# A pre-norm attention and mixture-of-experts layer: three output products taken in 32 bits, and the second norm of batch 0 turned by TensorE

## The chip, the cores and the metric

One Trainium2 chip; the kernel runs on one core of it. The metric is device time in microseconds (us) for one execution, the median of three runs.

## The reference

One transformer layer over `x` of 8 batches x 256 tokens x 256 features. Linear attention first, then a mixture of experts, each behind a layer norm:

```python
n = layernorm(x)
q, k, v = n @ Wq.T + bq, n @ Wk.T + bk, n @ Wv.T + bv
phi_q, phi_k = elu(q) + 1, elu(k) + 1
context = phi_q * cumsum(phi_k * v, axis=tokens) * 0.25
x = x + context @ Wo.T + bo
h = layernorm(x)
top2, idx = top_k(h @ router_w, 2);  scores = softmax(top2)
routed = sum over the two experts e of score * (silu(h @ w1g[e]) * (h @ w1u[e])) @ w2[e]
shared = silu(h @ w_gate) * (h @ w_up) @ w_down
out = x + routed + shared
```

There are 8 experts with an inner width of 512; the shared expert has 1024. All inputs and outputs are float32.

## The kernel before, in words

Every engine runs a list of steps in an order written out by hand; steps wait for each other on counting semaphores. A batch (index `i`, 0 to 7) is two tiles of 128 tokens. For each batch the steps are: first norm (`stats1`, `norm1`, `normed1`), turning the normed rows so that features lie on partitions, `project` (keys, values, queries), `exps` on ScalarE, `keys`, `sums` (the running sum), `queries` and `context` on VectorE, the output product `attend_out` on TensorE, `residual` on VectorE, second norm (`stats2`, `moments2`, GpSimd's `pow2`, VectorE's four small steps `newton2`, ScalarE's `normed2`), the turning of its result, `route` (router product), `gate_up` and `down` (the shared expert), `logits`, `ranks`, `slots`. `to_rows` scatters each token's row to a table in HBM. From about 195 us on the 36 expert blocks are worked through in one loop.

Products are made of float16 halves: each operand `a` is `a_h + a_l`, and a product is `a_h*w_h + a_h*w_l + a_l*w_h`. An output product of one batch, `attend_out(i)`, is therefore 12 matmuls of 256 columns, and its operand `cx` (the context, float32, stored in place over `rq`) must first be split: ScalarE writes `cx_h` (`context_hi`), VectorE subtracts and writes `cx_l` (`context_lo`). The attention weights lie in `wa_h` and `wa_l`, multiplied by `WS` = 64; their float32 original stays in `stage_att`.

The output bias `bo` is added to `xs` (the residual rows) by an accumulating DMA that GpSimd issues, `add_bo(i)`, for each batch ahead of `residual(i)`, which waits for it on `xbo0` or `xbo1`.

Turning: for batches 0 to 2 the first norm's rows are turned by TensorE (`turn_first`, then `turned_hi` on ScalarE and `turned_lo` on VectorE). All others, and the second norm of every batch, go as float16 halves (`row_hi2`, `row_lo`) through a DMA transpose that SP issues (`turn2`).

The head of the order, up to the first `route`, on TensorE is: `project(0)`, `project(1)`, 16 matmuls of ones that nobody reads (`warm(16)`), `attend_out(0)`, `turn_first(2)`, `project(2)`, `warm(10)`, `attend_out(1)` with a `warm(10)` inside, `warm(22)`, `route(0)`, `gate_up(0, 0)`. SP's queue holds `turn2(0)` ahead of the loads of the first three expert parts.

Of the kernel before, what the change touches and what calls it, by code (L numbers as in the profile page):

```python
# [26 lines left out]
P = 128  # L27
# [5 lines left out]
def layer_kernel(nc, x, w_att, w_bias, w_bo, w_shared, w_expert, out):  # L33
# [33 lines left out]
    with ExitStack() as ctx:  # L67
# [23 lines left out]
        def router_w(w):  # L91
# [15 lines left out]
        row_f = sb("row_f", [P, 1])  # L107
        spare = sb("spare", [P, 1])

# [103 lines left out]
        lent_down = lent[:, 2 * W1:2 * EW].rearrange("p (c s n) -> p c s n", s=2, n=D)  # L213
        ya = [xs[:, n, :] for n in range(NY)]

        names = """x0_in x1_in x2_in x_in att_k_in att_k_hi att_k_lo att_v_in att_v_hi att_v_lo att_in bias_in bo_in up_in gate_in down_in
            ex_in0 ex_in1 ex_in2 att_hi att_lo sh_hi sh_lo ex_hi ex_lo
            const_pool const_dve bias_done out_saved
            first0 first1 ln1_step pln ln2_step mv1_done ve1 ve2 pln2 float_done pow1 pow2 norm1_done norm2_done xn1 xn2 xbo0 xbo1
            t1 h1_done l1_done xT1_in h2_done l2_done xT2_in  # L220
# [47 lines left out]

        ON_DVE = 4


# [62 lines left out]
        def _(sp):  # L334
# [45 lines left out]

            turn2(0)
            for p in range(3):
# [75 lines left out]
        def _(pool):  # L458
# [182 lines left out]
            pool.wait_ge(S["bo_in"], 16)  # L641
            add_bo(0)
            add_bo(1)
# [139 lines left out]
        def _(pe):  # L783
# [47 lines left out]
            def attend_out(i):  # L831


                pe.wait_ge(S["cxh_done"], i + 1)
                if i >= 1:
                    pe.wait_ge(S["x1_done"], i)
                wh, wl = att_w(wa_h, 3), att_w(wa_l, 3)
                for s, (a, w) in enumerate(((cx_h, wh), (cx_h, wl), (cx_l, wh))):
                    if s == 2:
                        if i == 1:  # L840
                            warm(10)
                        pe.wait_ge(S["cxl_done"], i + 1)
                    for t in range(TB):
                        for k in range(KC):
                            ins = pe.matmul(bT[:, t * D:(t + 1) * D], a[:, k, t * P:(t + 1) * P], w[:, k, :],  # L845
                                            start=s + t + k == 0, stop=s == 2 and k == KC - 1, skip_group_check=True)
                ins.then_inc(S["wo_ps"], 1)

            def route(i):

                pe.wait_ge(S["xT2_in"], 16 * TB * (i + 1))
# [111 lines left out]
            warm(10)  # L963
# [13 lines left out]
            project(3, "k")  # L977
            attend_out(2)
            project(3, "qv")
# [149 lines left out]
        def _(act):  # L1129
            def exps(i, which="kq"):  # L1130

                for name, ready, e, r, m, ed, rd, used in (("k", "k_ps", ek, rk, 1, "ek_done", "rk_done", "kvs_done"),
                                                           ("q", "q_ps", eq, rq, 0, "eq_done", "rq_done", "cxl_done")):
                    if name not in which:
                        continue
                    src = projected(i, name)
                    act.wait_ge(S[ready], i + 1)
                    if i >= 1:
                        act.wait_ge(S[used], i)
                    for c in range(KC):  # L1140
                        act.activation(e[:, c, :], src[:, c * L:(c + 1) * L], ACT.Exp, bias=bias[:, m, c:c + 1],
                                       scale=1.0 / WS).then_inc(S[ed], 1)
                    for c in range(KC):
                        act.activation(r[:, c, :], src[:, c * L:(c + 1) * L], ACT.Identity, bias=bias1[:, m, c:c + 1],
                                       scale=1.0 / WS).then_inc(S[rd], 1)

            def load_exp():
                act.activation(spare[:], bias[:, 0, 0:1], ACT.Exp)

            def load_silu():  # L1150
                act.activation(spare[:], bias[:, 0, 0:1], ACT.Silu)

            def context_hi(i):
                act.wait_ge(S["cx_done"], i + 1)
                if i >= 1:
                    act.wait_ge(S["wo_ps"], i)
                act.activation(cx_h[:], cx, ACT.Copy).then_inc(S["cxh_done"], 1)
# [18 lines left out]
            def turned_hi(i):  # L1176

                act.wait_ge(S["t1"], i + 1)
                if i == 2:
                    act.wait_ge(S["q_ps"], 1)  # L1180
                act.activation(turned1(i)[:, 0:KC, :].rearrange("p k l -> p (k l)"), turn_bank(i)[:], ACT.Copy
                               ).then_inc(S["h1_done"], 1)

            def normed2(i):

                act.wait_ge(S["norm2_done"], 2 * (i + 1))
                if i >= 1:
                    act.wait_ge(S["l2_done"], i)
# [6 lines left out]
            def row_hi2(i):  # L1195
                act.wait_ge(S["xn2"], TB * (i + 1))
                if i >= 2:
                    act.wait_ge(*saved_before(i))
                    act.wait_ge(S["xT2_in"], 16 * TB * (i - 1))
                act.activation(rows2[i % 2][:, :, 0:D], xn[1][:], ACT.Copy).then_inc(S["h2_done"], 1)  # L1200
# [82 lines left out]
            load_exp()  # L1283
            context_hi(2)
            act_hi(0, 3)
# [134 lines left out]
        def _(dve):  # L1420
# [76 lines left out]
            def keys(i):  # L1497

                dve.wait_ge(S["ek_done"], KC * (i + 1))
                dve.wait_ge(S["rk_done"], KC * (i + 1))  # L1500
                dve.scalar_tensor_tensor(out=phik, in0=ek, scalar=1.0, in1=rk, op0=ALU.min, op1=ALU.max
                                         ).then_inc(S["phik_done"], 1)
                dve.wait_ge(S["phik_done"], i + 1)
                dve.wait_ge(S["v_ps"], i + 1)
# [25 lines left out]
            def context_lo(i):  # L1530
                dve.wait_ge(S["cxh_done"], i + 1)
                dve.tensor_tensor(cx_l[:], cx, cx_h[:], ALU.subtract).then_inc(S["cxl_done"], 1)

            def residual(i):

                dve.wait_ge(S["wo_ps"], i + 1)
                dve.wait_ge(S[f"xbo{i % 2}"], 16 * (i // 2 + 1))
                dve.scalar_tensor_tensor(out=xs_of(i), in0=bT[:].rearrange("p (t d) -> p t d", t=TB), scalar=1.0 / (WS * CS),
                                         in1=xs_of(i), op0=ALU.mult, op1=ALU.add).then_inc(S["x1_done"], 1)
# [88 lines left out]
            def turned_lo(i):  # L1628
                dve.wait_ge(S["h1_done"], i + 1)
                dve.tensor_tensor(turned1(i)[:, KC:2 * KC, :].rearrange("p k l -> p (k l)"), turn_bank(i)[:],  # L1630
                                  turned1(i)[:, 0:KC, :].rearrange("p k l -> p (k l)"), ALU.subtract).then_inc(S["l1_done"], 1)

            turned_lo(0)
            att_lo(slice(KC * D, 2 * KC * D), "att_v_hi", "att_v_lo")
# [58 lines left out]
            logits(1, 0)  # L1693
            context_lo(2)
            logits(1, 1)
# [263 lines left out]
```

## Time and profile before

| what | value |
|---|---|
| time, median of 3 runs (lowest to highest) | 355.33 us (355.15 to 355.61) |
| the profiled execution's own time | 356.11 us |
| its span, first to last instruction | 354.1 us |
| mean granted TensorE clock over the span | 0.996 |
| busy: TensorE / VectorE / ScalarE / GpSimd | 340.8 / 236.5 / 215.1 / 195.2 us |

Busy is the time an engine had an instruction in work; idle time of an engine counts only where another one waits for it. The span leaves out some 2.0 us of the profiled execution that lie around the first and last instruction.

### The profile page before, as it was taken

What the parts mean: (1) busy time and instruction counts of PE and PEld (TensorE: products, weight loads), DVE (VectorE), ACT (ScalarE), POOL (GpSimd) and SP (SyncE); (2) the same over time, 40 slices, a digit from 0 to 9 for tenths busy, and PEclk for the clock granted to TensorE, in tenths of its full rate; (3) what the DMA queues carried; (4) which work ended last, traced back from release to release, by engine and by line L of the source; (5) the groups of instructions that cost most, each with busy time, mean ns of one, the idle gap of its engine ahead of it and who ended that gap; (6) DMA issues with size and microseconds to landing.
All of it is one profiled execution on the core that took longest, in us unless ns stands there. A gap on an engine that the chain in (4) does not pass through costs nothing.

```text
span 354.1 us, 9236 instructions
## 1 busy us (share of the span) xinstructions
PE 340.8 (96%) x2971; PEld 257.5 (73%) x2971; DVE 236.5 (67%) x587; ACT 215.1 (61%) x391; POOL 195.2 (55%) x282
## 2 busy tenths in 40 slices
PE   7988989999999999999999999999999999999993
PEld 7877868888888898898988465656655556666662
DVE  4978998899989888887788554454544543334441
ACT  3669858787897977856536354454545544554551
POOL 4768986767785848356056444343443535443335
PEclk9999999999999999999999999999999999999998
DMA  7985342456774755725785346866496775765650
GB/s 197 381 213 103 137 108 45 132 144 209 128 228 105 140 185 136 197 92 152 234 266 134 91 76 98 105 86 92 68 114 94 89 113 80 104 106 90 94 71 8
DMA packets 77468, 46.43 MB, mean 131 GB/s; under 512 B 61040, under 2 KB 72560, under 8 KB 77040
## 3 DMA queue, kind: packets, MB, share of 16 engines
q1 hardware_dynamic: 63088, 35.08, 40.5%
q0 software_dynamic: 9664, 10.71, 19.0%
q10 hardware_dynamic: 4672, 0.07, 0.9%
q8 instruction: 26, 0.43, 0.5%
q14 instruction: 18, 0.15, 0.2%
HBM read 19.09 MB, written 12.97 MB: 91 GB/s over the span
## 4 chain that ended last, share of the span: by engine, by line
PE 73%; DVE 10%; DMA 6%; issue 4%; ACT 3%; POOL 1%; SPq 1%; POOLq 0%; DVEq 0%; ACTq 0%
PE bU L1065 13%; PE bG L1065 13%; PE bD L942 8%; PE bQ L1090 6%; PE bV L1090 6%; PE bG L238 6%; PE bU L238 6%; DMA xs<-bo 3%; PE bK L238 3%; PE bV L238 3%; PE bK L1045 2%; DMA bo<-in_w_bo 2%; DVE ab L1547 2%; PE bT L942 2%; PE bT L845 2%
## 5 line engine op out<-in xcount | busy, mean ns | idle before, releaser
L1547 DVE SCALAR_TENSOR_TENSOR ab<-bU,sg 128x512 f32<-128x512 f32 x64 | 44.1, 690 | 66.2 <-PE bU L1065 47.2
L773 POOL DMA_INDIRECT out_y<-xs,dst_row x32 | 49.6, 1551 | 60.1 <-DVE dst_row L1880 26.4
L1207 ACT ACTIVATE sg<-bG 128x512 f32<-128x512 f32 x64 | 37.9, 593 | 44.0 <-PE bG L1065 27.0
L1065 PE MATMUL bG<-we,work 128*128 (+1 forms) x216 | 52.6, 380 | 0.0
L1065 PE MATMUL bU<-we,work 128*128 (+1 forms) x216 | 52.6, 379 | 0.0
L571 POOL DMA_INDIRECT x_rows<-rows,slot_u x32 | 40.7, 1273 | 18.2 <-issue 10.7
L1374 ACT ACTIVATE ws_h<-ab 128x512 f16<-128x512 f32 x36 | 22.7, 629 | 41.6 <-DVE ab L1547 41.6
L1865 DVE TENSOR_TENSOR ws_h<-ab,ws_h 128x512 f16<-128x512 f32 x36 | 24.9, 692 | 20.8 <-ACT ws_h L1374 20.2
L1214 ACT ACTIVATE ah<-ab 128x512 f16<-128x512 f32 x32 | 20.1, 629 | 25.4 <-DVE ab L1547 21.3
L1065 PEld LDWEIGHTS bG<-we,work 128*128 128x128 f16 (+1 forms) x216 | 20.7, 99 | 19.3 <-issue 1.6
L1065 PEld LDWEIGHTS bU<-we,work 128*128 128x128 f16 (+1 forms) x216 | 19.9, 99 | 17.3
L1090 PE MATMUL bQ<-wd,ws_l 128*128 (+1 forms) x216 | 26.8, 273 | 0.1
L1090 PE MATMUL bV<-wd,ws_l 128*128 (+1 forms) x216 | 26.8, 273 | 0.0
L1090 PEld LDWEIGHTS bQ<-wd,ws_l 128*128 128x128 f16 (+1 forms) x216 | 21.0, 99 | 7.0 <-issue 1.9
L1090 PEld LDWEIGHTS bV<-wd,ws_l 128*128 128x128 f16 (+1 forms) x216 | 21.1, 99 | 6.7 <-issue 1.7
L768 POOL DMA_INDIRECT out_y<-xs,half_dst x8 | 12.3, 1543 | 23.9 <-issue 13.1
L238 PE MATMUL bG<-xT,ws_h 128*128 128x256 f16 x144 | 24.5, 273 | 0.0
L238 PE MATMUL bU<-xT,ws_h 128*128 128x256 f16 x144 | 24.5, 273 | 0.0
L1552 DVE TENSOR_TENSOR al<-ab,ah 128x512 f16<-128x512 f32 x32 | 21.7, 679 | 1.9 <-ACT ah L1214 1.8
L1381 ACT ACTIVATE ws_l<-bK 128x512 f16<-128x512 f32 x36 | 21.3, 592 | 0.6 <-PE bK L1045 0.6
L1603 DVE SCALAR_TENSOR_TENSOR we<-stage,we 128x1024 f16<-128x1024 f32 x16 | 19.5, 1219 | 0.8 <-ACT we L1234 0.8
L1045 PEld LDWEIGHTS bK<-ident,ws_h 128*128 128x128 f16 x144 | 10.6, 98 | 9.9 <-issue 1.6
(327 smaller groups left out, 822.4 us busy)
## 6 DMA issues: line engine op xcount, KB each, us to landing
stage<-in_w_expert SPq DMA_DIRECT2D x24, 512.0 KB
we<-in_w_shared SPq DMA_DIRECT2D x3, 1024.0 KB, 12.6
xs<-bo POOLq DMA_DIRECT2D x8, 256.0 KB, 4.3
out_y<-xs SPq DMA_DIRECT2D x8, 256.0 KB
xs<-in_x SPq DMA_DIRECT2D x1, 1280.0 KB, 19.4
x_rows<-we SPq DMA_DIRECT2D x9, 134.0 KB
xs<-in_x SPq DMA_DIRECT2D x3, 256.0 KB, 4.1
work<-x_rows SPq DMA_TRANSPOSE x40
```

The source lines that it names most:

```text
L238: ins = pe.matmul(dst, a(c), b(c), start=s == 0 and c == 0, stop=s == 2 and c == n - 1)
L571: pool.indirect_dma_start(xrows, bass.IndirectOffsetOnAxis(ap=slot_u[q][:, k, t:t + 1], axis=0), rows2[q][:, t, :].bitcast(U16), None).the ...
L773: pool.indirect_dma_start(out_rows, bass.IndirectOffsetOnAxis(ap=dst_row[:, b:b + 1], axis=0), ya[b % NY], None, bounds_check=NT * P - 1, ...
L942: ins = pe.matmul(dst[:, t * D:(t + 1) * D], a[:, at:at + P], w[:, 2 * f + c, :], start=f + s + t + c == 0, stop=f == NP - 1 and s == 2 an ...
L1065: ins = pe.matmul(dst[t * n:(t + 1) * n, :], x2[:, hi * KC + k, t * n:(t + 1) * n], w[t][lo][:, k, half, :], start=s == 0 and k == 0, stop ...
L1090: ins = pe.matmul(dst[t * m:(t + 1) * m, :], a[:, c, t * m:(t + 1) * m], w[t][:, c, lo, :], start=s == 0 and c == 0, stop=s == 2 and c == ...
L1207: act.activation(sg[q][:], src[:], ACT.Silu, scale=1.0 / WS).then_inc(S["sg_done"], 1)
L1374: act.activation(ar_h[n], ab[b % 2][:], ACT.Copy).then_inc(S["ah_done"], 1)
L1381: act.activation(aT_h[n].rearrange("p c l -> p (c l)"), bK[:], ACT.Copy).then_inc(S["ath_done"], 1)
L1547: dve.scalar_tensor_tensor(out=ab[q][:], in0=src[:], scalar=1.0 / WS, in1=sg[q][:], op0=ALU.mult, op1=ALU.mult).then_inc(S["a_done"], 1)
L1552: dve.tensor_tensor(al[f][:], ab[f % 2][:], ah[f][:], ALU.subtract).then_inc(S["al_done"], 1)
L1865: dve.tensor_tensor(ar_l[n], ab[b % 2][:], ar_h[n], ALU.subtract).then_inc(S["al_done"], 1)
```

## The change

The output products of batches 0, 1 and 2 are made from the unsplit float32 `cx` and the float32 weights in `stage_att`: 4 matmuls instead of 12 (`attend_whole`). Their `context_hi` and `context_lo` go. Batch 0's bias is laid into the same accumulator by two matmuls of one row (`add_bo_first`), in place of its accumulating DMA. Batch 0's second norm is turned by TensorE (`turn_second`), ScalarE (`turned2_hi`) and VectorE (`turned2_lo`) instead of the DMA transposes; its float16 rows are still written for `to_rows`. The order of the head follows on every engine. `WHOLE` is 3.

```diff
@@ SP's queue
-            turn2(0)
             for p in range(3):
                 load_part(p)
             turn2(1)
@@ GpSimd
             pow1(0)
+            pool.memset(cs_row, CS).then_inc(S["cs_row"], 1)
...
-            add_bo(0)
             add_bo(1)
             norm1(2)
@@ TensorE, new functions
+            def add_bo_first():
+                pe.wait_ge(S["bo_in"], 16)
+                pe.wait_ge(S["cs_row"], 1)
+                pe.wait_ge(S["l1_done"], 2)
+                for t in range(TB):
+                    pe.matmul(bT[:, t * D:(t + 1) * D], cs_row, bo[0:1, :], start=t == 0, stop=False, skip_group_check=True)
+
+            def attend_whole(i):
+                pe.wait_ge(S["att_in"], 16)
+                pe.wait_ge(S["cx_done"], i + 1)
+                if i >= 1:
+                    pe.wait_ge(S["x1_done"], i)
+                w = att_w(stage_att, 3)
+                for t in range(TB):
+                    for k in range(KC):
+                        ins = pe.matmul(bT[:, t * D:(t + 1) * D], cx[:, k, t * P:(t + 1) * P], w[:, k, :],
+                                        start=i >= 1 and t + k == 0, stop=k == KC - 1, skip_group_check=True)
+                ins.then_inc(S["wo_ps"], 1)
+
+            def turn_second():
+                pe.wait_ge(S["xn2"], TB)
+                pe.wait_ge(S["rq_done"], KC * 2)
+                for t in range(TB):
+                    for k in range(KC):
+                        ins = pe.transpose(bD[:, k * L + t * P:k * L + (t + 1) * P], xn[1][:, t, k * P:(k + 1) * P], ident[:])
+                ins.then_inc(S["t2"], 1)
@@ TensorE, order
             project(1)
-            warm(16)
-            attend_out(0)
+            add_bo_first()
+            warm(4)
+            attend_whole(0)
             turn_first(2)
             warm(8, bQ)
-            project(2)
-            warm(10)
-            attend_out(1)
-            warm(22)
+            project(2, "kv")
+            turn_second()
+            project(2, "q")
+            attend_whole(1)
             route(0)
             pe.wait_ge(S["const_pool"], 6)
             gate_up(0, 0)
+            warm(24, bD)
             gate_up(0, 1)
...
             project(3, "k")
-            attend_out(2)
+            attend_whole(2)
             project(3, "qv")
@@ ScalarE, exps: a later batch's queries wait for the product that reads cx
-                    if i >= 1:
+                    if i >= 1 and name == "k":
                         act.wait_ge(S[used], i)
+                    elif 1 <= i <= WHOLE:
+                        act.wait_ge(S["wo_ps"], i)
+                    elif i > WHOLE:
+                        act.wait_ge(S[used], i - WHOLE)
@@ ScalarE, order
             exps(1, "k")
-            context_hi(0)
             normed1(2)
             turned_hi(2)
-            exps(1, "q")
             act.wait_ge(S["up_in"], 16)
             shared_hi(1, 0)
+            exps(1, "q")
             normed2(0)
             row_hi2(0)
-            context_hi(1)
+            turned2_hi()
             act.wait_ge(S["down_in"], 16)
             shared_hi(2, 0)
             exps(2, "k")
-            shared_hi(0, 1)
             exps(2, "q")
             silu(0, 0)
-            shared_hi(1, 1)
+            shared_hi(0, 1)
             act_hi(0, 0)
             silu(1, 1)
+            shared_hi(1, 1)
             normed2(1)
...
-            context_hi(2)
@@ VectorE, order (keys is cut into mapped_keys and key_values)
             context(0)
-            context_lo(0)
-            keys(1)
+            shared_lo(0, 0)
+            mapped_keys(1)
             residual(0)
             stats2(0)
             moments2(0)
+            key_values(1)
             turned_lo(2)
-            sums(1)
             for k in range(4):
                 newton2(0, k)
+            sums(1)
             queries(1)
             context(1)
+            turned2_lo()
+            shared_lo(1, 0)
             row_lo(1, 0)
-            shared_lo(0, 0)
-            context_lo(1)
-            shared_lo(1, 0)
             dve.wait_ge(S["x_in"], 16)
...
             logits(0, 2)
+            shared_lo(2, 0)
             swiglu(0, 0)
-            shared_lo(2, 0)
...
-            context_lo(2)
```

## Rows read from the trace of the kernel before

**Rows 1.** Stretch, busy us of PE, PEld, DVE, ACT, POOL, granted clock, DMA share, GB/s.

```profile
20.00:30.00 10.00, 7.81 (x84) 6.76 (x82) 7.97 (x19) 6.29 (x13) 6.67 (x17) 1.00 0.64 156
...
54.00:64.00 10.00, 10.00 (x98) 8.64 (x97) 9.33 (x25) 8.38 (x18) 6.37 (x15) 1.00 0.30 52
...
195.00:345.00 150.00, 149.59 (x1087) 90.36 (x1086) 70.08 (x206) 74.07 (x141) 63.40 (x57) 1.00 0.65 92
345.00:355.00 10.00, 3.40 (x31) 2.38 (x28) 1.38 (x2) 1.90 (x4) 4.62 (x3) 0.82 0.10 11
```

**Rows 2.** TensorE's waits from 54 us on: total us, times, longest.

```profile
PE bK L1045 <- ACT ws_h L1374: 0.4, 2, 0.2
```

**Rows 3.** The chain that ended last, to 60 us: start, us, what.

```profile
12.11 10.21 DMA xs<-bo
...
24.80 1.75 POOL y L511
...
31.23 2.51 DMA xT<-rows
```

**Rows 4.** Timeline of TensorE: start, length, line, tiles, count, idle before.

```profile
18.33 1.06 PE L786 MATMUL bR<-ones 128*128 128x128 f16 x16
...
20.94 0.60 PE L795 MATMUL bR<-ident,xn 128*128 128x128 f32 x4
...
34.10 1.03 PE L909 MATMUL bG<-xT,ws_h 128*128 128x256 f16 x8
...
50.85 0.39 PE L238 MATMUL bK<-xT,wa_h 128*128 128x256 f16 x2 [0.83 <-DMA xT<-rows]
...
52.52 0.61 PE L845 MATMUL bT<-wa_h,cx_h 128*128 128x256 f16 x4 [0.18 <-ACT cx_h L1157]
...
53.84 0.38 PE L238 MATMUL bQ<-xT,wa_h 128*128 128x256 f16 x2
```

**Rows 5.** Groups by shape: count, busy us, mean ns of one, idle before.

```profile
L795 PEld LDWEIGHTS bT<-ident,xn 128*128 128x128 f32 x8 | 0.8, 141 | 0.6 <-DVE xn L1456 0.6
```

**Rows 6.** Timeline of VectorE.

```profile
18.05 0.69 DVE L1527 SCALAR_TENSOR_TENSOR work<-work 128x512 f32<-128x512 f32 x1
...
22.42 0.69 DVE L1538 SCALAR_TENSOR_TENSOR xs<-bT,xs 128x512 f32<-128x512 f32 x1 [0.62 <-DMA xs<-bo]
...
24.81 1.22 DVE L1512 TENSOR_TENSOR_SCAN work<-keep,work 128x512 f32<-128x512 f16 x1
26.57 0.16 DVE L1472 SCALAR_TENSOR_TENSOR nt<-y 128x2 f32<-128x2 f32 x1 [0.55 <-POOL y L511]
...
29.14 0.69 DVE L1495 TENSOR_TENSOR rows<-xn,rows 128x512 f16<-128x512 f32 x1 [0.48 <-ACT rows L1200]
29.75 1.22 DVE L1609 SCALAR_TENSOR_TENSOR ws_l<-we,ws_h 128x1024 f16<-128x1024 f32 x1
30.89 0.68 DVE L1532 TENSOR_TENSOR cx_l<-work,cx_h 128x512 f16<-128x512 f32 x1
...
36.99 0.69 DVE L1547 SCALAR_TENSOR_TENSOR ab<-bU,sg 128x512 f32<-128x512 f32 x1 [0.64 <-PE bU L909]
...
45.38 0.73 DVE L1492 TENSOR_TENSOR rows<-xn,rows 128x512 f16<-128x512 f32 x1 [0.28 <-ACT rows L1174]
...
51.11 0.69 DVE L1527 SCALAR_TENSOR_TENSOR work<-work 128x512 f32<-128x512 f32 x1
```

**Rows 7.** Timeline of ScalarE.

```profile
36.24 1.05 ACT L1238 ACTIVATE ws_h<-we 128x1024 f16<-128x1024 f32 x1
37.71 0.63 ACT L1214 ACTIVATE ah<-ab 128x512 f16<-128x512 f32 x1 [0.42 <-DVE ab L1547]
...
39.54 1.09 ACT L1192 ACTIVATE xn<-xs,shift,rstd 128x256 f32<-128x256 f32 x2 [0.71 <-DVE shift L1486]
```

**Rows 8.** Timeline of GpSimd.

```profile
36.89 0.71 POOL L511 TENSOR_TENSOR y<-ve,minus_half 128x2 f32<-128x2 f32 x1
```

More of the change, by code:

```diff
@@ L107, in layer_kernel @@
         row_f = sb("row_f", [P, 1])
-        spare = sb("spare", [P, 1])
+        spare = sb("spare", [P, 2])
         xs = sb("xs", [P, NT, D])
@@ L214, in layer_kernel @@
         ya = [xs[:, n, :] for n in range(NY)]
+        cs_row = sg[1][0:1, 0:P]
         names = """x0_in x1_in x2_in x_in att_k_in att_k_hi att_k_lo att_v_in att_v_hi att_v_lo att_in bias_in bo_in up_in gate_in down_in
@@ L218, in layer_kernel @@
             const_pool const_dve bias_done out_saved
-            first0 first1 ln1_step pln ln2_step mv1_done ve1 ve2 pln2 float_done pow1 pow2 norm1_done norm2_done xn1 xn2 xbo0 xbo1
+            first0 first1 ln1_step pln ln2_step mv1_done ve1 ve2 pln2 float_done pow1 pow2 norm1_done norm2_done xn1 xn2 xbo0 xbo1 cs_row t2 h2_turned l2_turned
             t1 h1_done l1_done xT1_in h2_done l2_done xT2_in
@@ L269, in layer_kernel @@
         ON_DVE = 4
+        WHOLE = 3
         def ln2_at(i):
@@ L847, in attend_out @@
                 ins.then_inc(S["wo_ps"], 1)
-            def route(i):
-                pe.wait_ge(S["xT2_in"], 16 * TB * (i + 1))
+            def add_bo_first():
[8 more added lines that the diff above has]
+                if i >= 1:
+                    pe.wait_ge(S["x1_done"], i)
+                w = att_w(stage_att, 3)
[11 more added lines that the diff above has]
+                ins.then_inc(S["t2"], 1)
+            def route(i):
+                if i == 0:
+                    pe.wait_ge(S["h2_turned"], 1)
+                    pe.wait_ge(S["l2_turned"], 1)
+                else:
+                    pe.wait_ge(S["xT2_in"], 16 * TB * i)
                 if i >= 1:
@@ L1147, in load_exp @@
             def load_exp():
-                act.activation(spare[:], bias[:, 0, 0:1], ACT.Exp)
+                act.activation(spare[:, 0:1], bias[:, 0, 0:1], ACT.Exp)
             def load_silu():
-                act.activation(spare[:], bias[:, 0, 0:1], ACT.Silu)
+                act.activation(spare[:, 1:2], bias[:, 0, 0:1], ACT.Silu)
             def context_hi(i):
                 act.wait_ge(S["cx_done"], i + 1)
-                if i >= 1:
+                if i > WHOLE:
                     act.wait_ge(S["wo_ps"], i)
@@ L1182, in turned_hi, with turned2_hi @@
                                ).then_inc(S["h1_done"], 1)
+            def turned2_hi():
+                act.wait_ge(S["t2"], 1)
+                act.activation(xT2[0][:, 0:KC, :].rearrange("p k l -> p (k l)"), bD[:], ACT.Copy).then_inc(S["h2_turned"], 1)
             def normed2(i):
                 act.wait_ge(S["norm2_done"], 2 * (i + 1))
+                if i == 1:
+                    act.wait_ge(S["t2"], 1)
                 if i >= 1:
@@ L1198, in row_hi2 @@
                     act.wait_ge(*saved_before(i))
-                    act.wait_ge(S["xT2_in"], 16 * TB * (i - 1))
+                if i >= 3:
+                    act.wait_ge(S["xT2_in"], 16 * TB * (i - 2))
                 act.activation(rows2[i % 2][:, :, 0:D], xn[1][:], ACT.Copy).then_inc(S["h2_done"], 1)
@@ L1497, in keys, with mapped_keys @@
             def keys(i):
+                mapped_keys(i)
+                key_values(i)
+            def mapped_keys(i):
                 dve.wait_ge(S["ek_done"], KC * (i + 1))
@@ L1502, in keys, with key_values @@
                                          ).then_inc(S["phik_done"], 1)
+            def key_values(i):
                 dve.wait_ge(S["phik_done"], i + 1)
@@ L1530, in context_lo @@
             def context_lo(i):
-                dve.wait_ge(S["cxh_done"], i + 1)
+                dve.wait_ge(S["cxh_done"], i - WHOLE + 1)
                 dve.tensor_tensor(cx_l[:], cx, cx_h[:], ALU.subtract).then_inc(S["cxl_done"], 1)
@@ L1536, in residual @@
                 dve.wait_ge(S["wo_ps"], i + 1)
-                dve.wait_ge(S[f"xbo{i % 2}"], 16 * (i // 2 + 1))
-                dve.scalar_tensor_tensor(out=xs_of(i), in0=bT[:].rearrange("p (t d) -> p t d", t=TB), scalar=1.0 / (WS * CS),
+                if i >= 1:
+                    dve.wait_ge(S[f"xbo{i % 2}"], 16 * ((i + 1) // 2))
+                dve.scalar_tensor_tensor(out=xs_of(i), in0=bT[:].rearrange("p (t d) -> p t d", t=TB),
+                                         scalar=1.0 / (CS if i < WHOLE else WS * CS),
                                          in1=xs_of(i), op0=ALU.mult, op1=ALU.add).then_inc(S["x1_done"], 1)
@@ L1631, in turned_lo, with turned2_lo @@
                                   turned1(i)[:, 0:KC, :].rearrange("p k l -> p (k l)"), ALU.subtract).then_inc(S["l1_done"], 1)
+            def turned2_lo():
+                dve.wait_ge(S["h2_turned"], 1)
+                dve.tensor_tensor(xT2[0][:, KC:2 * KC, :].rearrange("p k l -> p (k l)"), bD[:],
+                                  xT2[0][:, 0:KC, :].rearrange("p k l -> p (k l)"), ALU.subtract).then_inc(S["l2_turned"], 1)
             turned_lo(0)
```

8 lines of the change are left out of this document (2 added, 6 removed).

## The prediction

> **What bounds the kernel now.** Read the busy time by stretch first. From 54 to 64 us TensorE is busy 10.00 of 10 us, in the expert loop 149.59 of 150 [rows 1], and its waits from 54 us on come to one entry of 0.4 us [rows 2]. From there the time is TensorE's work, so a change ahead of 54 us is worth what it shifts the moment at which this dense stream begins, plus what it takes out of the stream. From 20 to 30 us TensorE is busy 7.81 of 10, part of it with products of ones: the head is bound by a chain of small steps.
>
> The chain of waits shows it [rows 3]: batch 0's bias DMA takes 10.21 us from 12.11 and ends after the product it is added to; GpSimd's power takes 1.75; the DMA transpose 2.51. VectorE's row at 22.42 says the same: 0.62 idle, ended by that DMA [rows 6]. The dense part starts with `gate_up(0, 0)` at 34.10, but one last time TensorE waits on others: 0.83 for a transpose at 50.85 and 0.18 for ScalarE's `cx_h` at 52.52 [rows 4]. The end of `attend_out(2)`, 53.84, is therefore my yardstick.
>
> **The price of a 32-bit product.** No row has one. `attend_out(2)` runs 12 float16 matmuls of 256 columns from 52.52 to 53.84 [rows 4]: 0.11 us each, 1.32 in all. Lower bound: four 32-bit transposes of 128 columns took 0.60 us, what four float16 matmuls of 256 take (0.61, both with the tail of the last) [rows 4], so two passes over the columns, 0.22 for 256 columns, 0.88 for a product of four. Upper bound while passes alone count: a full product of two operands of two halves has four partial products where the split form has three, 1.32 x 4 / 3 = 1.76. Beyond that, weight loads: a 32-bit one took 141 ns [rows 5]; one for each of 16 passes, overlapped, makes 2.26, and not overlapped 16 x (0.11 + 0.141) = 4.0. I take 1.76: this is a true product, not a copy, and the row nearest to it is the split product. The bias's two matmuls are half of that, 0.88 (0.44 to 2.0). The Trainium skill (FP8 and Floating Point Precision, section TensorE Precision Notes) says that true FP32 makes four passes through the array; by it the product would be an estimated 1.76 as well, by the transposes' row 0.88; no run here shows it yet.
>
> **Batch 0's product and residual.** `warm(16)` starts at 18.33 and `context(0)` ends at 18.74 (18.05 + 0.69) [rows 4, 6]. New on TensorE: 18.33 + 0.88 (bias) + 0.22 (four products of ones; 16 took 1.06 with the tail) = 19.43, by when the context is there; + 1.76 = 21.19; + 0.17 tail and 0.06 to VectorE = 21.42. VectorE is free by 20.45 (18.66 + 1.14 `shared_lo` + 0.65 `mapped_keys`; starts follow one another 0.05 to 0.1 sooner than durations say). So `residual(0)` starts at 21.42 instead of 22.42: -1.00. The bias DMA alone would have allowed 1.2; the dearer product eats the rest.
>
> **The second norm.** The power starts 2.38 behind the residual (22.42 to 24.80), so at 23.80. It took 1.75 while VectorE's running sum (24.81, 1.22 long) was under way, and 0.71 beside a step that reads PSUM [rows 3, 6, 8]. In the new order `key_values(1)` and `turned_lo(2)` are there, both reading PSUM, and `sums(1)` stands behind `newton2`: I take 0.71, done at 24.52 (bounds 0.71 and 1.75). VectorE itself is free at 24.70: residual and statistics 1.82, two value steps 0.85, `turned_lo` 0.60. `newton2(0)` starts at 24.70 instead of 26.57: -1.87. The Trainium skill (SBUF — State Buffer, Who interferes with whom) says that a VectorE instruction with two SBUF inputs blocks a GpSimd instruction that reads SBUF; the row agrees. By that rule the power is free of it here, the -1.87; without it the sum would lose 1.04, less 0.18 of slack.
>
> **VectorE from there to `swiglu(0, 0)`.** Before: 26.57 to 36.99, 10.42 us, of it 0.48 and 0.64 idle [rows 6]. The order now holds, more: `sums(1)` 1.14, `turned2_lo` 0.60, `shared_lo(2, 0)` 1.14; less: `shared_lo(0, 0)` 1.14 (`shared_lo` from 29.75 to 30.89) and `context_lo(1)` 0.60. 10.42 - 1.12 + 1.14 = 10.44; start at 35.14: -1.85. The stretch must be free of waits. Its inputs: `xn` of batch 0 at 26.6 (25.5 + 1.1); TensorE turns it to 27.1, ScalarE's high half ends at 27.9; `context(1)` ends at 27.95: met. `attend_whole(1)` runs from 28.4 (project(2) ends) to 30.16; `residual(1)` is due at 31.3: 0.9 to spare. `gate_up(0, 0)` starts at 30.5 instead of 34.10, yet this is not the gain: `gate_up(0, 1)` needs `silu(0, 0)`, behind `exps(2)` on ScalarE, and `swiglu(0, 0)`. `warm(24)`, 1.3 us, fits in front of that and is hidden by it; without that cover it would cost 1.3.
>
> **To the products of batch 2.** ScalarE's `act_hi(0, 0)` stood 0.72 behind that `swiglu`; from it to `normed2(1)` were 1.83, 0.71 of them idle [rows 7]. Now no idle but `shared_hi(1, 1)`, some 0.95 of its 1.05: 2.07. The rest to `row_lo(0, 3)` (39.54 to 45.38) is unchanged: 35.14 + 0.72 + 2.07 + 5.84 = 43.77 instead of 45.38, -1.61. From there VectorE had no idle time to the end of `context(2)` at 51.80; it moves to 50.19. Then `context_hi(2)` and its handing over fall away (51.80 to 52.52, now 0.05: -0.67) and the product costs 1.76 for 1.32 (+0.44): it ends at 52.00, against 53.84. **-1.84.** The transposes of batch 3's first norm, issued 1.6 earlier and no longer queued behind others, end ahead of it: `project(3, "k")` 48.5 to 49.8. SP's queue loses `turn2(0)`, so the first three expert loads go out right behind the last x load; their data is used after 60 us, so I cost it at nothing. GpSimd loses one DMA issue and gains one memset, off the chain. Its `norm1(3)` and `pow2(1)` now run beside `shared_lo(2, 0)` and may end up to 1.2 later; `newton2(1)` would wait 0.7, which the slack ahead of `row_lo(0, 3)` mostly takes (0.2 in the range).
>
> Sum: -1.00 - 0.87 + 0.02 + 0.24 - 0.67 + 0.44 = -1.84. Span 354.1 to 352.3, profiled execution 356.11 to 354.3, median 355.33 to **353.5**; the profiled execution is 0.78 above the median, which I carry along.
>
> **Rivals.** (a) Two passes: residual bound by VectorE at 20.5 (-0.9 more), product 2 cheaper by 0.88: 351.7. For it: the transposes' row. (b) The power stays blocked, or another step slips: +1.0, 354.5. For it: VectorE has no idle time left to absorb slips. (c) The change doesn't pay: products bound by loads, 2.26; 0.5 and 0.25 (bias) into the chain, 0.5 into the stream: 354.7. (d) Slower: loads not overlapped, 4.0 a product. Extra e = 2.25 each: 1.5e on batch 0, e - 0.9 on batch 1, e on batch 2, +7.0: 360.5. It decides at e = 0.74, a product of 2.5 us; slower by 0.2% from 2.75. Against it: the f16 stream hides its loads. (e) The clock: 58 products of ones go, 28 come. The granted clock stood at 1.00 with 7.81 of 10 busy and was 0.82 in the stretch with 3.40 of 10 [rows 1]; my new head leaves one wait of some 0.8 us there, for `turned_lo(2)` (done at 24.76; TensorE is through the eight matmuls and twelve products of ones ahead of it at 24.0). A fall to the lower level (1.2 GHz) over `attend_whole(1)` and `gate_up(0, 0)` would double 4.4 us: with 2 to 3 of them on the chain 356.5. [...]
>
> **Numbers.** Forecast 0.53 (own range 352.8 to 354.2), (a) 0.08, (b) 0.15, (c) 0.11, (d) 0.07, (e) 0.06. Less than 0.2% (0.7 us) either way can't be told from no change. Range 351.6 to 355.2: all but (d), (e). Faster: forecast, (a), half of (b), 0.69. Same: the rest of (b), (c), 0.18. Slower 0.13.
>
> **What would show it.** `residual(0)` near 21.4 with TensorE as releaser; a power of 0.7; 32-bit matmuls 0.44 apart; `swiglu(0, 0)` near 35.1; `attend_whole(2)` ending near 52.0; no new wait of TensorE past 54; clock 1.00 from 20 to 50. I am wrong if a product passes 2.5 us, if VectorE shows idle time between 25 and 35, or if the lead at 52 is lost behind it.

## The result and the profile after

The changed kernel took 353.73 us (median of 6 runs, 353.48 to 354.46) against 355.33 (6 runs, 355.15 to 355.65) for the kernel before: 1.60 us less. The ratio of the two is 0.9956, with a 95% interval of [0.9943, 0.9968], so the gain is small but clear of the noise. The forecast was 353.5, with a range of 351.6 to 355.2. The profiled execution took 353.77 us with a span of 351.8 us (before: 356.11 and 354.1) at a granted clock of 0.997.

First the stretches (stretch, busy us of PE, PEld, DVE, ACT, POOL, granted clock, DMA share, GB/s), beside [rows 1]:

```profile
20.00:30.00 10.00, 9.24 (x79) 7.96 (x78) 8.33 (x19) 7.34 (x15) 6.86 (x17) 1.00 0.86 280
...
54.00:64.00 10.00, 10.00 (x107) 8.52 (x106) 9.16 (x22) 9.18 (x18) 7.88 (x15) 1.00 0.29 78
...
193.00:343.00 150.00, 149.59 (x1088) 90.31 (x1086) 69.98 (x207) 74.38 (x141) 63.37 (x58) 1.00 0.68 93
```

TensorE is busy 9.24 of 10 us in the head, where it was 7.81, and nothing is different in the dense part: 149.59 of 150 once more, a little earlier. Its waits past 54 us (total, times, longest), beside [rows 2]:

```profile
PE bK L1079 <- ACT ws_h L1418: 0.4, 2, 0.2
PE bD L974 <- issue: 0.2, 1, 0.2
```

So nearly all that was won was won ahead of 54 us. TensorE's timeline there, beside [rows 4]:

```profile
18.32 1.12 PE L853 MATMUL bT<-bo,sg 1*128 1x256 f32 x4
19.38 0.40 PE L787 MATMUL bR<-ones 128*128 128x128 f16 x4
19.61 1.95 PE L864 MATMUL bT<-wd,work 128*128 128x256 f32 x8
21.39 0.60 PE L796 MATMUL bR<-ident,xn 128*128 128x128 f32 x4
...
24.92 0.61 PE L823 MATMUL bK<-xT,wa_h 128*128 128x256 f16 x4 [0.52 <-DVE xT L1684]
...
26.70 0.66 PE L874 MATMUL bD<-ident,xn 128*128 128x128 f32 x4
...
28.50 1.89 PE L864 MATMUL bT<-wd,work 128*128 128x256 f32 x8
30.23 0.24 PE L239 MATMUL bR<-wa_h,xT 128*128 128x8 f16 x4
...
30.53 1.03 PE L941 MATMUL bG<-xT,ws_h 128*128 128x256 f16 x8
...
33.15 1.50 PE L787 MATMUL bD<-ones 128*128 128x128 f16 x24
...
48.68 0.39 PE L239 MATMUL bK<-xT,wa_h 128*128 128x256 f16 x2 [0.61 <-DMA xT<-rows]
...
50.00 1.91 PE L864 MATMUL bT<-wd,work 128*128 128x256 f32 x8
51.74 0.38 PE L239 MATMUL bQ<-xT,wa_h 128*128 128x256 f16 x2
```

The price that no row of before had is the distance between starts: 19.61 to 21.39, 28.50 to 30.23 and 50.00 to 51.74, so 1.78, 1.73 and 1.74 us for a product of four 32-bit matmuls. Each 32-bit matmul stands as two records (x8 for four), and each record takes the time of two float16 matmuls. The last line is the yardstick: the product of batch 2 ends at 51.74, against 53.84 [rows 4], 2.10 earlier.

The weight loads by shape (count, busy us, mean ns of one, idle before), beside [rows 5]:

```profile
L864 PEld LDWEIGHTS bT<-wd,work 128*128 128x128 f32 x24 | 4.3, 190 | 0.5
```

There are eight loads for a product, one for each record (24 for the three products), and not the 16 that the prediction's rival counted. A load takes 190 ns, eight of them 1.5 us, less than the 1.73 to 1.78 of the product: they lie under the matmuls. VectorE, beside [rows 6], and GpSimd, beside [rows 8]:

```profile
21.59 0.69 DVE L1591 SCALAR_TENSOR_TENSOR xs<-bT,xs 128x512 f32<-128x512 f32 x1 [1.27 <-PE bT L864]
...
24.78 0.15 DVE L1516 SCALAR_TENSOR_TENSOR nt<-y 128x2 f32<-128x2 f32 x1
...
35.17 0.68 DVE L1601 SCALAR_TENSOR_TENSOR ab<-bU,sg 128x512 f32<-128x512 f32 x1
36.48 0.16 DVE L1516 SCALAR_TENSOR_TENSOR nt<-y 128x2 f32<-128x2 f32 x1 [0.63 <-POOL y L512]
...
43.46 0.69 DVE L1536 TENSOR_TENSOR rows<-xn,rows 128x512 f16<-128x512 f32 x1 [0.57 <-ACT rows L1212]
```

```profile
23.98 0.72 POOL L512 TENSOR_TENSOR y<-ve,minus_half 128x2 f32<-128x2 f32 x1
...
34.03 1.31 POOL L498 TENSOR_SCALAR rstd<-neg 128x2 f32<-128x2 f32 x1
```

`residual(0)` is now released by TensorE and not by a DMA; the power takes 0.72 where it took 1.75 [rows 3]; `newton2(0)`, at 24.78, waits for nothing; and from there to `swiglu(0, 0)` at 35.17 VectorE works without a wait. Last, the chain that ended last (start, us, what; SPq is SyncE's queue), on its way to batch 2:

```profile
41.36 0.61 DVE rows L1539
...
41.99 1.31 SPq L375
43.35 1.25 SPq L375
44.72 1.19 SPq L365
45.95 2.52 DMA xT<-rows
48.68 1.48 PE bK L239 x12
50.16 1.74 PE bT L864 x8
```

The product of batch 2 does not start when its context is ready: VectorE's last step of `context(2)` starts at 49.15 and is 0.69 long, so it was ready at 49.84, and the product starts right behind `project(3, "k")`, which waited 0.61 for a DMA transpose. The transposes bind.

What starts them is read one step further back. L1539 is VectorE's `row_lo` of batch 1's second norm; as it ends, SyncE issues that norm's two transposes (L375), right behind them the two of batch 3's first norm (L365), and `project(3, "k")` goes 3.96 us after the start of that last pair of issues. It was the same in the kernel before:

```profile
44.20 2.51 SPq L373 DMA_TRANSPOSE xT<-rows  x2
46.83 2.52 SPq L363 DMA_TRANSPOSE xT<-rows  x2
```

From 46.83 to 50.85 are 4.02 us. So this input of batch 2's stretch follows VectorE's second norm of batch 1 and the SyncE queue, and not the first norm of batch 3, whose rows (43.46 + 0.69) are there before the queue is free at 44.60.

### The profile page after: what moved, and what is told of

It is laid out like the page before. It is cut to its first block, busy times and chain, and to the rows that moved or that the text cites. A ratio compares the mean times of both kernels' runs of the same rounds, so it can differ in the third digit from the quotient of the medians.

```text
span 351.8 us, 9162 instructions
## 1 busy us (share of the span) xinstructions
PE 340.8 (97%) x2937; PEld 256.8 (73%) x2937; DVE 235.0 (67%) x585; ACT 214.0 (61%) x389; POOL 193.4 (55%) x282
## 4 chain that ended last, share of the span: by engine, by line
PE 83%; DVE 7%; POOL 2%; DMA 2%; issue 2%; SPq 1%; ACT 1%; POOLq 0%; DVEq 0%; ACTq 0%
PE bU L1099 13%; PE bG L1099 13%; PE bD L974 9%; PE bU L239 9%; PE bG L239 8%; PE bQ L1124 6%; PE bV L1124 6%; PE bV L239 4%; PE bK L239 3%; PE bK L1079 2%; PE bQ L239 2%; PE bT L974 2%; PE bT L843 1%; PE bT L864 1%; DVE ws_l L1663 1%
## 5 line engine op out<-in xcount | busy, mean ns | idle before, releaser
L572 POOL DMA_INDIRECT x_rows<-rows,slot_u x32 | 41.6, 1301 | 18.2 <-issue 10.7
```

Of the source, the lines that this page charges most:

```text
L572: pool.indirect_dma_start(xrows, bass.IndirectOffsetOnAxis(ap=slot_u[q][:, k, t:t + 1], axis=0), rows2[q][:, t, :].bitcast(U16), None).the ...
```

## The experiments

Three sets of four kernels, each timed beside the kernel before on the same chip, whose medians were 355.62, 355.43 and 355.29 (21, 22 and 30 runs). Gains are read as ratios; 0.001 is 0.36 us, and an interval reaches some 0.3 to 0.6 us to either side. A profile is of one execution, which can lie anywhere in the scatter of its kernel; where that matters it is said.

**The changed kernel once more (`after_again`).**

> The changed kernel, unedited, beside the kernel before on the chip of the runs that follow. Theory: the ratio of the first result, 0.9956. Rival, after the kernel without the 24 products of ones came out at 0.9976 although its TensorE stream reached the expert loop no later (193.17 against 193.30 us): the difference is one between chips or executions, and this one gives 0.997 or more as well.

353.90 us, 0.9956 [0.9943, 0.9969]: the same ratio in another set. It is the measure for all that follows.

**Batch 0's bias by DMA again (`bias_by_dma`).** The rest of the change stays.

```diff
             pool.wait_ge(S["bo_in"], 16)
+            add_bo(0)
             add_bo(1)
...
-            add_bo_first()
-            warm(4)
+            warm(16)
             attend_whole(0)
```

> The changed kernel with batch 0's bias added by the accumulating DMA again, as in the kernel before (16 products of ones in place of the bias matmuls and the four). Theory: residual(0) sets the head's pace and waits for that DMA, so it starts near 22.3 instead of 21.59 and the whole loss reaches the end: 354.4 (353.73 + 0.7). Rival: the head's gain comes from the power and from the order behind it, and the residual's start has slack: no more than 0.2, 353.9.

353.84 us, 0.9950 [0.9937, 0.9964]: no loss that the runs can tell, where I had expected 0.7. VectorE's timeline shows why:

```profile
21.68 0.69 DVE L1590 SCALAR_TENSOR_TENSOR xs<-bT,xs 128x512 f32<-128x512 f32 x1 [1.06 <-DMA xs<-bo]
```

The DMA binds `residual(0)`, as before, but lands by 21.6 and not by 22.3 [rows 3], so the residual starts 0.09 later than with the bias on TensorE. The bias matmuls hold TensorE for 1.06 us in front of the product; without them it starts at 19.08 and waits at its end for the DMA instead, which comes to nearly the same.

**The bias part alone (`bias_alone`)**, put into the kernel before, with its row scaled for the split product:

```diff
-            add_bo(0)
             add_bo(1)
...
             project(1)
-            warm(16)
+            add_bo_first()
             attend_out(0)
```

> The kernel before with the bias part alone: batch 0's bias comes from two 32-bit matmuls of one row ahead of the split product (in place of the 16 products of ones), its accumulating DMA goes. Prediction's view: the DMA held residual(0) to 22.42; now VectorE takes it at 21.75, behind keys(1): 0.6 faster, 354.8. Rival: in most executions the DMA lands near 21.6, as it did at 21.63 in the changed kernel with the DMA put back, and the 22.32 of the profile is one execution's: 0.2 or less, 355.3.

354.60 us, 0.9982 [0.9973, 0.9991]: 0.6 us faster than before.

```profile
23.95 1.74 POOL L512 TENSOR_TENSOR y<-ve,minus_half 128x2 f32<-128x2 f32 x1
```

`residual(0)` starts at 21.58, and the power still takes 1.74 us. So the same part is worth 0.6 us when put into the kernel before and nothing that can be told when taken out of the changed one. The profiles differ in when the DMA lands: by 22.3 in that of before, by 21.6 in that of `bias_by_dma`, and in `power_free` below, with the DMA of before, `residual(0)` starts at 22.10 without waiting for it. That the landing explains the 0.6 is argued, not shown, and why it moves was not followed.

**The power's neighbour alone (`power_free`)**, in the kernel before: VectorE's running sum of two SBUF inputs goes behind the norm that waits for the power.

```diff
-            sums(1)
             for k in range(4):
                 newton2(0, k)
+            sums(1)
```

> The kernel before with one step moved: VectorE's running sum of batch 1, sums(1), stands behind the four steps of newton2(0) instead of ahead of them. Theory: GpSimd's power (24.80) no longer runs beside a VectorE step with two inputs in SBUF and takes 0.7 instead of 1.75; the second norm of batch 0 ends 1.0 earlier and 0.7 to 1.0 of it reaches the end: 354.5. Rival: the head's gain comes from the bias, the products or the turning, not from this; 0.2 or less, 355.3.

```profile
24.47 0.72 POOL L511 TENSOR_TENSOR y<-ve,minus_half 128x2 f32<-128x2 f32 x1
```

The power fell from 1.75 [rows 3] to 0.72 by one moved VectorE step; with the 1.74 of the run above, where that step stood in its old place, that settles what the power waits for. It is what the Trainium skill (SBUF — State Buffer, Who interferes with whom) says of a VectorE instruction with two SBUF inputs and a GpSimd instruction that reads SBUF. The kernel took 354.77 us, 0.9990 [0.9981, 0.9999], 0.4 us faster for a step 1.03 shorter, less than the 0.7 to 1.0 that I had expected, and only just clear of no change. In the profile TensorE's last two waits were 0.65 for a transpose at 49.78 and 0.36 for ScalarE at 51.63, not shorter in sum than in [rows 4], but earlier.

**Batch 0's second norm turned by DMA again (`turn_by_dma`)**, without the two `turned2` steps on ScalarE and VectorE.

```diff
+            turn2(0)
             for p in range(3):
                 load_part(p)
...
-            turn_second()
             project(2, "q")
             attend_whole(1)
+            warm(24, bR)
             route(0)
...
-            warm(24, bD)
```

> The changed kernel with batch 0's second norm turned by the DMA transposes again; 24 products of ones stand ahead of route(0) instead of behind gate_up(0, 0). Theory: VectorE and GpSimd bound the stretch, TensorE has slack there. route(0) moves from 30.2 to about 32.6, swiglu(0, 0) by 0.6 at most, but newton2(1) still waits for GpSimd's power at 36.45: 0 to 0.4 slower than the changed kernel, 353.7 to 354.1. Rival: turning by TensorE is what brings the gain: 1.5 or more slower, 355.3, as gate_up(0, 0) is lost to 32.9.

354.79 us, 0.9978 [0.9969, 0.9987]: 0.8 us slower than the changed kernel, more than the 0 to 0.4 that I had expected of it. TensorE's timeline has the waits:

```profile
32.93 0.26 PE L239 MATMUL bR<-wa_h,xT 128*128 128x8 f16 x4 [1.08 <-DMA xT<-rows]
...
49.99 0.39 PE L239 MATMUL bK<-xT,wa_h 128*128 128x256 f16 x2 [0.95 <-DMA xT<-rows]
```

The router starts at 32.93 instead of 30.23, and `swiglu(0, 0)` at 36.13 instead of 35.17, 0.96 later, of which 0.48 is a head that began late in this execution (its bias matmuls start at 18.80, not 18.32). I had taken the four 128-column transposes on TensorE to buy nothing, since VectorE binds that stretch; they buy some 0.5 there, because with the DMA `gate_up(0, 0)` comes too late for VectorE (a wait of 0.54 for bU). At `project(3, "k")` the profile is 1.31 late: SyncE issues batch 3's pair 0.86 later (45.58), and from there to TensorE it takes 4.41 instead of 3.96.

**Batch 2's product in its split form (`batch2_split`).**

```diff
-        WHOLE = 3
+        WHOLE = 2
...
-            attend_whole(2)
+            attend_out(2)
```

> The changed kernel with batch 2's output product from float16 halves again (WHOLE = 2; context_hi(2) and context_lo(2) back in their places). Theory: that product waits for TensorE, busy until 50.0 behind a DMA transpose, and only 0.16 less for the context; with the split it starts near 50.5 and ends near 51.85 instead of 51.74: 353.8. Prediction's sum: 0.23 later, 353.95. Rival: the step on ScalarE and the 0.6 on VectorE are worth their full 1.2: 354.9.

354.02 us, 0.9960 [0.9946, 0.9973]: 0.1 us, as expected and no more than the runs can tell. The split product waits 0.39 for ScalarE's high half and takes 1.32; the whole one waits for nothing and takes 1.74.

```profile
50.83 0.61 PE L843 MATMUL bT<-wa_h,cx_h 128*128 128x256 f16 x4 [0.39 <-ACT cx_h L1195]
```

**No products of ones before `gate_up(0, 1)` (`no_warm24`).**

```diff
             gate_up(0, 0)
-            warm(24, bD)
             gate_up(0, 1)
```

> The changed kernel without the 24 products of ones behind gate_up(0, 0). Theory: they are hidden, since gate_up(0, 1) needs silu(0, 0) (33.97) and its second half swiglu(0, 0) (35.85): no change, 353.7 within 0.2. Rival A: they sit on the path, 0.5 or more faster. Rival B: they hold the clock; the granted clock falls below 1.00 after 33 us and the time grows by 1 or more.

354.61 us (11 runs, 354.11 to 355.33), 0.9976 [0.9967, 0.9985]: 0.7 us slower for leaving out work, though the two intervals just touch. Its profile does not show the loss, and it can hardly do so, for the profiled execution is the fastest of the eleven (354.11): `project(3, "k")` starts at 48.66 and the expert loop at 193.17, where the changed kernel has 48.68 and 193.30. Three of its 11 executions had a mean granted clock of 0.994, a value that none of the eleven of the changed kernel had (0.995 to 0.999), and these three were above the median.

**Ones given back elsewhere (`no24_filled`)**: the same, and

```diff
+            warm(20, bQ)
             project(3, "k")
```

> The changed kernel without the 24 products of ones behind gate_up(0, 0), with 20 in front of project(3, k) instead, where TensorE waits 0.6 for a DMA transpose. Clock theory: without the 24 the kernel was slower (354.61 against 353.9) because the granted clock falls in some executions when TensorE waits, first for silu(0, 0) and then for the transposes; with the second wait filled it is back at 353.9, within 0.2, plus at most 0.5 where the products outlast the wait. Rival: the 24 hold back something else that then collides; no change against 354.6.

354.07 us (6 runs, 353.87 to 354.34), 0.9968 [0.9956, 0.9979], clocks 0.997 to 0.999. Though twenty products of ones now stand on the path (`project(3, "k")` starts at 49.12, 0.44 later), 0.3 us comes back by the ratios, and the scatter shrinks from 1.2 us (11 runs) to 0.5 (6 runs). The intervals overlap, so the clock as the cause of the loss in `no_warm24` fits but is not shown.

**32 more products of ones in front of batch 0's product (`delay32`).**

```diff
-            warm(4)
+            warm(36)
             attend_whole(0)
```

> The changed kernel with 36 products of ones ahead of attend_whole(0) instead of 4, 1.76 us more in front of it. Theory: batch 0's product, residual and second norm set the pace of all that follows up to 50 us, so 1.5 to 1.8 slower than the changed kernel. Rival: another chain (ScalarE's copies, GpSimd's constants, the transposes) has caught up, 0.5 or less slower; then what the bias DMA or the product costs did not matter either.

356.31 us, 1.0019 [1.0010, 1.0028]: 2.2 us slower than the changed kernel, for 1.76 us of ones and an expectation of 1.5 to 1.8.

```profile
24.04 0.69 DVE L1591 SCALAR_TENSOR_TENSOR xs<-bT,xs 128x512 f32<-128x512 f32 x1 [3.06 <-PE bT L864]
```

This execution's head was 0.65 late before the ones (18.97, not 18.32), and 0.65 + 1.76 = 2.41 is what `residual(0)` (2.45) and the product of batch 2 (52.44, 2.44) are late. So the whole delay of batch 0's product passes to the yardstick: nothing between has slack. The expert loop starts 3.00 late (196.30). Of the other 0.6 (3.00 less 2.41) TensorE's timeline has 0.43 as one wait, of a later `project` at 119.26, for a DMA transpose, which the changed kernel does not have.

**`project(1, "q")` behind batch 0's product (`q_later`)**, so that the product starts when its context is ready.

```diff
-            project(1)
+            project(1, "kv")
             add_bo_first()
-            warm(4)
             attend_whole(0)
             turn_first(2)
-            warm(8, bQ)
+            project(1, "q")
```

> The changed kernel with batch 1's query projection moved behind attend_whole(0) and turn_first(2), where it replaces 8 products of ones; the 4 ahead of the product go as well. The product then starts when the context is there (18.65) instead of at 19.61, and residual(0) at 20.7 instead of 21.6. Theory: 0.7 to 0.9 faster than the changed kernel, all of it passed on. Rival: the stretch behind it is bound by something else, within 0.2 of the changed kernel.

```profile
18.97 1.96 PE L864 MATMUL bT<-wd,work 128*128 128x256 f32 x8 [0.60 <-DVE work L1578]
...
48.04 0.39 PE L239 MATMUL bK<-xT,wa_h 128*128 128x256 f16 x2 [0.60 <-DMA xT<-rows]
...
49.36 1.92 PE L864 MATMUL bT<-wd,work 128*128 128x256 f32 x8
```

The product starts 0.64 earlier, and so do `project(3, "k")` and the product of batch 2: here the transposes of batch 3 were issued 0.63 earlier (44.09) and landed earlier by as much. But the median is 353.62, 0.9950 [0.9937, 0.9963], 0.2 to 0.3 us less than the changed kernel, where I had expected 0.7 to 0.9, and within the interval. TensorE's waits from 62 to 100 us, in which the changed kernel has none:

```profile
PE bR L239 <- DMA xT<-rows: 1.0, 1, 1.0
```

The lead is lost to a later transpose (at 83.47), and the expert loop starts at 193.34, not 193.30: being early at 54 us is worth only what the stream behind it can use.

**That, and VectorE's `shared_lo(2, 0)` behind `swiglu(0, 0)`, with 8 ones instead of 24 (`both`).**

```diff
-            shared_lo(2, 0)
             swiglu(0, 0)
+            shared_lo(2, 0)
...
-            warm(24, bD)
+            warm(8, bD)
```

> As the kernel with the later query projection, and shared_lo(2, 0) back behind swiglu(0, 0) on VectorE, with 8 instead of 24 products of ones behind gate_up(0, 0). Theory: in the changed kernel VectorE idles 0.63 for GpSimd's power, which shared_lo(2, 0) holds up (1.31 for a 0.26 step), and ScalarE 0.96 for swiglu(0, 0); both go, 0.4 to 0.8 on top, 1.3 to 1.6 faster than the changed kernel. Rival: DMA transposes of batches 1 and 3 or TensorE's own work bound it, no more than the later query projection alone.

355.22 us (12 runs, 353.67 to 359.71), 0.9992 [0.9976, 1.0009]: the whole gain gone, where I had expected 0.4 to 0.8 more. The ratio leaves the 359.71 out, and without it the median is 355.00. The profiled execution is one of the slow end (356.68). TensorE:

```profile
48.88 0.39 PE L239 MATMUL bK<-xT,wa_h 128*128 128x256 f16 x2 [1.87 <-DMA xT<-rows]
49.34 1.06 PE L239 MATMUL bK<-xT,wa_h 128*128 128x256 f16 x4
...
51.05 2.71 PE L864 MATMUL bT<-wd,work 128*128 128x256 f32 x8
```

and the two stretches around them (columns as in the first fence):

```profile
46.00:50.00 4.00, 2.13 (x16) 1.30 (x15) 3.86 (x11) 0.58 (x1) 3.38 (x4) 0.91 0.42 121
50.00:54.00 4.00, 4.00 (x18) 3.19 (x17) 0.41 (x3) 1.62 (x5) 1.22 (x2) 0.66 0.54 100
```

A wait of 1.87 us in a stretch with 2.13 of 4 us busy, and the granted clock fell: four float16 matmuls that take 0.60 at 2.4 GHz take 1.06, and 0.66 over four microseconds means that most of them passed at 1.2 GHz. The product of batch 2 takes 2.55 (51.05 to 53.60) instead of 1.74. Five of the six executions above the median had mean clocks of 0.987 to 0.994.

The step moved on VectorE did not bring its 0.63 either:

```profile
35.67 0.16 DVE L1515 SCALAR_TENSOR_TENSOR nt<-y 128x2 f32<-128x2 f32 x1 [0.61 <-POOL y L512]
```

With `shared_lo(2, 0)` behind `swiglu(0, 0)`, GpSimd's `rstd` step takes 0.25 again, but now batch 1's power, from 33.89, runs beside `shared_lo(2, 0)` and takes 1.74 instead of 0.71. `newton2(1)` waits 0.61 for it all the same and starts only 0.18 earlier than in `q_later` (35.85). It is the mechanism of `power_free` once more, at another step.

**The same with 20 ones into that wait (`both_filled`).**

```diff
+            warm(20, bQ)
             project(3, "k")
```

> The kernel with both reorderings (355.22 median, executions from 353.7 to 359.7, granted clock 0.66 from 50 to 54 us in its profile) with 20 products of ones in front of project(3, k). Clock theory: the clock stays at 1.00 from 46 to 54 us, the scatter of the executions shrinks to 1 us and the median falls to 353.3 or less. Rival: the long wait for the transposes, 1.87, is itself the loss and stays; 354.5 or more.

354.12 us (12 runs, 353.79 to 355.49), 0.9971 [0.9961, 0.9980]. The same two stretches, and TensorE's first matmul behind the ones:

```profile
46.00:50.00 4.00, 3.23 (x39) 2.63 (x37) 3.85 (x11) 0.62 (x1) 3.38 (x4) 1.00 0.41 120
50.00:54.00 4.00, 4.00 (x32) 3.48 (x30) 1.88 (x7) 2.16 (x7) 1.18 (x2) 1.00 0.56 104
...
48.86 0.39 PE L239 MATMUL bK<-xT,wa_h 128*128 128x256 f16 x2 [0.77 <-DMA xT<-rows]
```

Twenty products of ones, a microsecond's work, go with a clock of 1.00 and take 0.7 us off by the ratios. Eleven of the twelve executions of `both` lie at 354.46 or more, ten of these twelve at 354.43 or less. The transposes release TensorE at the same moment in the two profiles (48.88 and 48.86), so the wait is not what differs; the product of batch 2 ends at 51.91 instead of 53.60. Between these two kernels the clock is shown as the cause of the difference. The forecast of 353.3 or less was missed all the same, and the other half says why: `project(3, "k")` starts 0.18 later than in the changed kernel, though SP issued its transposes some 0.8 earlier. In `both`:

```profile
41.18 2.60 SPq L375 DMA_TRANSPOSE xT<-rows  x2
43.90 2.54 SPq L365 DMA_TRANSPOSE xT<-rows  x2
```

From the second pair's issue to TensorE are 4.98 us here and 4.99 in `both_filled`, against 3.96 in the changed kernel, 3.95 in `q_later` (which issued the pair only 0.19 later than `both`) and 3.93 in `delay32`. So an earlier issue does bring earlier transposes in `q_later` and does not in these two; what holds them up by a microsecond lies behind SP's queue and was not found. No version beat the changed kernel by more than its interval.

## Why the prediction came out

**What bounds.** Right. The time is the start of the dense stream plus the stream: 2.10 us won by the end of batch 2's product and 2.26 by the expert loop (195.56 to 193.30), of a span 2.3 shorter. `delay32` shows it from the other side. `q_later` sets a limit to it: a lead of 0.64 at 50 us was gone by the expert loop.

**The 32-bit product.** Taken at 1.76 from the bound of four partial products; 1.73 to 1.78 measured. Rivals (a), two passes, (c), bound by loads at 2.26, and (d), loads not overlapped at 4.0, fall with this one number. A load is dearer than the row that I had (190 ns, not 141), but there are 8 of them and not the 16 of rivals (c) and (d): 1.52 us, which stay hidden.

**Batch 0's residual.** 21.42 forecast, 21.59 measured, -0.83 instead of -1.00. The mis-sized term is the two bias matmuls: 0.88 taken as half a product, 1.06 measured. A single row of weights makes such a matmul no cheaper than a full one; here it was dearer.

**The power and `newton2(0)`.** 0.71 and 24.70 forecast, 0.72 and 24.78 measured; `power_free` and `bias_alone` show its cause by themselves. Rival (b) falls.

**VectorE's stretch.** `swiglu(0, 0)` at 35.14 forecast, 35.17 measured, without a wait between. This sum was nearly exact because it counted steps in a stretch in which one engine binds. The worry, `newton2(1)` held by GpSimd, came as priced (0.63; the `rstd` step took 1.31 beside `shared_lo(2, 0)`, which starts with it at 34.03). The slack ahead of `row_lo(0, 3)` took it, as I had said: 43.46 measured, 43.77 forecast. But that is not the branch that bound: `newton2(1)` lies ahead of batch 1's `row_lo`, which starts the transposes, and no slack stands there.

**Batch 2.** Right in size, wrong in what ends last. I wrote that the transposes "end ahead of it" and that the context binds: `context(2)` was done at 49.84 (50.19 forecast), but the transposes let `project(3, "k")` go only at 48.68 (48.5 forecast), which put the product at 50.00. I also had them "no longer queued behind others": they are issued right behind batch 1's pair, as before. That the transposes moved by 2.17 (50.85 to 48.68) and the context by 1.96, nearly alike, is because both follow the same stretch of VectorE. 0.16 us decide which of them binds, and that the product's end, 51.74, came within 0.26 of the 52.00 with the wrong branch is in part luck. That it matters is seen in `both`, where more lead on VectorE found the transposes where they were.

**The clock.** Rival (e) did not come: 1.00 from 20 to 64 us. But "`warm(24)` is hidden" was only half of it. It does lie beside other work; leaving it out costs 0.7 us nevertheless, for a reason that is not shown, and where a wait of 1.87 us does open the clock falls (0.66 in `both`). Products of ones whose time is covered can still have a worth.

**From span to median.** The step that failed in size. The profiled execution of before lay 0.78 above its median, and I carried this along; the one of after lies 0.04 above. The spans of the two profiled executions differ by 2.3, the medians by 1.60. The spans of before's other executions were mostly 353.2 to 353.9, those of the changed kernel's six 351.7 to 352.5: the profiled execution of before was one of the longer ones. One thing late in it may be the bias DMA: it lands by 22.3 there, and in `power_free`, with the same DMA, the residual starts at 22.10 without waiting for it. That is argued, not shown. The profiled execution gained 2.34, 0.50 more than the forecast's 1.84, and the 0.78 carried along was 0.04, 0.74 less; what is left of the two errors is the 0.24 by which the gain in the medians falls short. That the 353.5 came so near owes something to their opposite signs.

**What each part is worth.** Undone one at a time in the changed kernel: turning 0.8, batch 2's whole product 0.1, the bias nothing (a ratio 0.0006 lower, in the noise). Done alone in the kernel before: the bias 0.6, the power's order 0.4. These add to no sum; each moves what the next one waits for. No run splits the products of batches 0 and 1 again in the changed kernel, so what the 32-bit products are worth by themselves is not measured, but for the last of the three. The bias and the power's order, done alone, need none of them; the two were not run together.

**Open.** Why the transposes of batch 3 take a microsecond longer in `both` and `both_filled`; why the bias is worth 0.6 in one kernel and nothing in the other; what the whole products of batches 0 and 1 bring; and in which stretch `no_warm24` loses its 0.7.

## What to carry to other kernels

Price an operation that the profile lacks by counting passes of the nearest rows, count its loads too, and see whether they stay hidden; then follow the one engine that binds step by step, where such a sum came out to 0.03 us here. At the point where the streams meet, list every input with its own time and what started it, queues included, not only the one that was last before: here two were 0.16 us apart, and they changed places. A step moved out of the way of a slow neighbour can fall beside the next one, as the power of batch 1 did in `both`: look at what the other engine does at the new time. And judge a part by undoing it in the final kernel as well as by doing it alone in the first, for the two can differ by its whole worth.

## What the hardware showed that was not expected

- A 32-bit matmul of 128x128 by 256 columns takes 0.43 to 0.44 us, as two records, and its weight loads 190 ns each, all hidden; a 32-bit transpose of 128 columns is one record of 0.11 us with a load of 140 ns. The Trainium skill (FP8 and Floating Point Precision, TensorE Precision Notes) has four passes for true FP32; the product agrees (1.74 against 1.32 for three), the transposes take half of that for their columns.
- Two 32-bit matmuls with a single row of weights took 1.06 us (18.32 to 19.38), 0.53 each: more than the full ones.
- In `both` the granted clock fell after one wait of 1.87 us (0.91, then 0.66 over the next 4 us), and twenty products of ones of 128 columns in that wait kept it at 1.00.
- Two pairs of DMA transposes issued 0.81 us earlier released TensorE 0.20 later in `both` (48.88 against 48.68); issued 0.63 earlier in `q_later`, they released it 0.64 earlier.
- A GpSimd power of 128x2 took 1.74 us beside a VectorE step with two inputs in SBUF in three profiles (24.80 in before, 23.95 in `bias_alone`, 33.89 in `both`), and 0.71 to 0.72 without.
